# Last matrix products and their sums in halves, gate by a sigmoid on ScalarE, and the first tile's gather of 38 rows as 36 and 2

## Chip, cores and metric

One Trainium2 chip, one of its cores. The metric is the device time in microseconds of one execution; smaller is better. A measurement gives the median of several runs.

## What is computed

The kernel is one block of a vision transformer over 32 images of 36 patches, with 2 class rows ahead of each image's patches: 38 rows of 256 values an image. Cut to what matters here, for the second half of the block (`xn` is the normalised input, twice over):

```python
abel_out = gelu(xn @ abel_w + abel_b)
logits = xn @ moe_gate_w + moe_gate_b
topw, topi = top_k(logits, 2); topw = softmax(topw)
eo = gelu(xn @ ew1[e] + eb1[e]) @ ew2[e] + eb2[e]        # for the two experts of a row
moe_out = sum of topw * eo
for i in range(3):
    moe_out = moe_out @ expm(gens[i])                    # 256 x 256 rotations
gate = sigmoid(concat([abel_out, moe_out]) @ gc_w + gc_b)
out = residual + abel_out * (1 - gate) + moe_out * gate
```

## The kernel before

All engines run programs of their own, written out by hand and tied by semaphores; the order on each engine is the order of its code. The rows are cut into 11 tiles (`NT`) of 3 images, 114 rows; the last tile has 2 images, 76 rows. The class rows are alike in every image, so they are computed once, with image 0.

The work comes in stages: embedding of the patches, attention, the expert choice, and then 25 slots (`NS`) of 128 rows, each for one expert. GpSimd gathers a slot's rows, PE multiplies by the expert's two matrices, VectorE adds the bias (L1230), and GpSimd scatters the result to `y_rows` in HBM (L510). Beside the slots the three matrix exponentials are computed by polynomial and repeated squaring, in the buffers `Y` and `YT` (transposed), each 128 x 512: two row blocks of 256 columns.

The change touches what comes behind the slots. There:

- **SP** (L385 to L408) waits until all slots' results are in `y_rows`, then issues the gathers into `qk_sb` (L396): one per image, in order of tiles, 32 in all. Each takes 36 rows of 2 KB, both experts' results side by side, save image 0, whose transfer takes all 38 rows. Each tile has a semaphore `d_gather[t]`. Behind the last gather SP issues the outputs: for tile t it waits for `out_set` and issues a transfer per image (L401), and after tile 0 one more (L407) that writes the class rows of the other 31 images. Those are 33. At the end SP waits for all of them.
- **PE** finishes the exponentials by four products in a row (L1685 to L1690, the function `product`, whose matrix instructions have line L1559): the last square of exponential 2 into bank 4, the last square of exponential 1 (held transposed) into bank 0, their product into bank 4, and its product with exponential 0 into bank 5. Each is 4 matrix instructions, 8 passes in the profile, since 32-bit values take two. Then, per tile, `turn_moe` (L1698) transposes the weighed rows into bank 0 or 1, and `rotate` (L1709, L1711) multiplies by the product of the exponentials into one of banks 2 to 5 and subtracts `abel_out`. A 257th column gives the gate's argument; for tile 0 it is made by two more instructions (L1716), because `rotate(0)` begins before that column is set.
- **VectorE** adds, in `rotation` (L1244 to L1262): the two squares (L1245, L1248), the first product's sum (L1252), then the second weighing of tile 0's rows (`weigh_both`, L1288), the last sum into `ywide_sb` (L1256), and the gate column (L1260). Then, per tile, in `rotated`: it bounds the gate's argument (L1296), weighs the rows of tile t + 3 (L1288), and after ScalarE's exponential adds 1 and inverts (L1300, L1301), and computes `gate * (moe - abel) + (residual + abel)` (L1302).
- **ScalarE** loads the table of the exponential (L763), weighs the first expert's rows (`weigh_first`, L766) of tiles 0, 1 and 2, copies tile 0's transposed rows out of PSUM (`keep_moeT`, L755), and then goes round per tile: weigh tile t + 3, copy tile t + 1, exponential for the gate of tile t (L760).

## Time and profile before

| | us |
|---|---|
| runs | 341.42, 341.82, 345.4 |
| median | 341.82 |
| profiled execution, its own time | 344.48 |
| its span, first to last instruction | 341.6 |
| PE busy | 317.0 (93%) |
| VectorE busy | 209.5 (61%) |
| ScalarE busy | 183.4 (54%) |
| GpSimd busy | 148.4 (43%) |

The span leaves out 2.88 us of the profiled execution that lie around it. Busy times are sums over the whole span; issuing a DMA doesn't count as busy, so SP has no share there, and its queue is to be seen in the timeline only, as `SPq`. A mean granted TensorE clock of 0.989 stands beside this span.

### The profile page before, as it was taken

Reading aid. Unit: us, or ns where it says so; the run is one execution under the profiler, and the core shown is the slowest. Engines: PE = TensorE matmul, PEld = TensorE weight load, DVE = VectorE, ACT = ScalarE, POOL = GpSimd, SP = SyncE. Lnnn points to the kernel's source line nnn. Section 1 sums busy time; section 2 is a strip of 40 time slices with the busy share of each in tenths; the row PEclk is TensorE's granted clock in tenths of the full one; section 3 lists DMA queues with packets and bytes.
Section 4 is the critical chain, followed back from the end, with each engine's and each line's share of the span. In section 5 each row is a group of like instructions: output and inputs, shape, how many; then the busy total and the mean of one; then the engine's idle time right before and its main releaser. Section 6 shows DMA issues by size and latency. Waiting matters only on the chain.

```text
span 341.6 us, 6400 instructions
## 1 busy us (share of the span) xinstructions
PE 317.0 (93%) x1944; PEld 267.8 (78%) x1944; DVE 209.5 (61%) x576; ACT 183.4 (54%) x427; POOL 148.4 (43%) x152
## 2 busy tenths in 40 slices
PE   5999899999796999989999899999999999998894
PEld 4888455578685998876788788899998999896682
DVE  0146668599999688898877468776312231113684
ACT  0111454899798479975662594243443655550451
POOL 2002547133888468583002267857761654422000
PEclk9999999999999699999999999999999999999999
DMA  7940511124111111008834366636352466632632
GB/s 233 359 165 8 225 59 56 54 72 157 46 47 46 47 45 45 18 2 308 327 132 133 97 186 177 178 111 179 118 180 77 142 197 220 188 107 86 178 110 82
DMA packets 19219, 44.40 MB, mean 130 GB/s; under 512 B 2549, under 2 KB 11316, under 8 KB 18934
## 3 DMA queue, kind: packets, MB, share of 16 engines
q1 hardware_dynamic: 16790, 37.48, 33.8%
q0 software_dynamic: 2400, 6.56, 6.1%
q8 instruction: 15, 0.25, 0.3%
q14 instruction: 14, 0.11, 0.1%
HBM read 36.94 MB, written 7.09 MB: 129 GB/s over the span
## 4 chain that ended last, share of the span: by engine, by line
PE 75%; DVE 13%; DMA 3%; issue 3%; ACT 2%; POOL 1%; SPq 1%; DVEq 0%; POOLq 0%; ACTq 0%
PE banks L1611 11%; PE banks L1620 10%; PE banks L1559 10%; PE banks L1322 8%; PE banks L1459 5%; PE banks L1363 4%; PE banks L1435 4%; PE banks L1709 3%; PE banks L1477 2%; PE banks L1407 2%; PE banks L1421 2%; PE banks L1530 2%; PE banks L1368 2%; DVE kc_sb L917 2%; DVE qk_sb L1179 2%
## 5 line engine op out<-in xcount | busy, mean ns | idle before, releaser
L1611 PE MATMUL banks<-qn_sb,w_sb 128*128 128x128 f32 x400 | 49.1, 276 | 1.6 <-issue 0.8
L1611 PEld LDWEIGHTS banks<-qn_sb,w_sb 128*128 128x128 f32 x400 | 46.7, 192 | 2.4 <-issue 1.5
L1620 PE MATMUL banks<-w_sb,sq_sb 128*128 x200 | 47.1, 379 | 0.0
L694 ACT ACTIVATE qn_sb<-banks,col_sb 128x128 f32<-128x128 f32 x50 | 20.2, 457 | 44.2 <-PE banks L1598 44.2
L504 POOL DMA_INDIRECT qn_sb<-z_rows,gidx_sb x25 | 26.9, 1076 | 35.9 <-DVE gidx_sb L1133 18.9
L510 POOL DMA_INDIRECT y_rows<-pT_sb,sidx_sb x25 | 24.8, 991 | 39.8 <-DVE pT_sb L1230 38.9
L1230 DVE TENSOR_TENSOR pT_sb<-banks,p_sb 128x256 f32<-128x256 f32 x25 | 10.6, 424 | 49.7 <-PE banks L1620 46.9
L1620 PEld LDWEIGHTS banks<-w_sb,sq_sb 128*128 128x128 f32 x200 | 36.7, 190 | 4.3
L705 ACT ACTIVATE sq_sb<-banks,col_sb 128x128 f32<-128x128 f32 x100 | 31.2, 366 | 12.6 <-PE banks L1611 12.3
L592 ACT ACTIVATE kc_sb<-banks,col_sb 32x152 f32<-32x152 f32 x66 | 31.0, 470 | 1.1
L1322 PE MATMUL banks<-patch_sb,wtok_sb 128*128 128x252 f32 (+1 forms) x120 | 26.9, 388 | 3.7 <-DMA wtok_sb<-in_w_tok 3.7
L1322 PEld LDWEIGHTS banks<-patch_sb,wtok_sb 128*128 128x128 f32 x120 | 23.1, 207 | 6.7 <-DMA wtok_sb<-in_w_tok 4.0
L917 DVE TENSOR_SCALAR kc_sb<-banks,col_sb 32x152 f32<-32x152 f32 x66 | 25.6, 424 | 2.9 <-PE banks L1421 2.4
L297 POOL TENSOR_TENSOR qn_sb<-qk_sb,wtok_sb 114x768 f32<-114x768 f32 x11 | 17.1, 1556 | 14.7 <-DVE wtok_sb L892 7.6
L1459 PEld LDWEIGHTS banks<-vd_sb,pT_sb 114*114 114x114 f32 x132 | 18.3, 184 | 6.1 <-issue 5.4
L1459 PE MATMUL banks<-vd_sb,pT_sb 114*114 114x147 f32 x132 | 20.7, 300 | 2.1 <-ACT pT_sb L606 2.1
L583 ACT ACTIVATE qd_sb<-banks,col_sb 32x304 f32<-32x304 f32 x33 | 19.7, 597 | 4.0 <-PE banks L1407 3.6
L1363 PE MATMUL banks<-wqkv_sb,h_sb 128*114 128x512 f32 x44 | 20.8, 594 | 0.5 <-DVE wqkv_sb L838 0.5
L1435 PE MATMUL banks<-kc_sb,qd_sb 96*114 96x76 f32 x176 | 20.5, 262 | 0.0
L1435 PEld LDWEIGHTS banks<-kc_sb,qd_sb 96*114 96x114 f32 x176 | 20.4, 184 | 0.0
L474 POOL TENSOR_TENSOR att_sb<-p_sb 114x256 f32<-114x256 f32 x11 | 8.2, 745 | 25.8 <-DVE p_sb L970 25.8
L463 POOL TENSOR_TENSOR vd_sb<-vrep_sb,con_sb 114x768 f32<-114x768 f32 x11 | 17.1, 1551 | 0.0
(235 smaller groups left out, 632.1 us busy)
## 6 DMA issues: line engine op xcount, KB each, us to landing
w_sb<-in_w SPq DMA_DIRECT2D x25, 512.0 KB, 3.8
w_sb<-in_w SPq DMA_DIRECT2D x1, 4096.0 KB, 12.4
vrep_sb<-v_rows SPq DMA_DIRECT2D x33, 114.0 KB
qk_sb<-y_rows SPq DMA_DIRECT2D x31, 72.0 KB
patch_sb<-in_patches SPq DMA_DIRECT2D x2, 756.0 KB, 5.6
patch_sb<-in_patches SPq DMA_DIRECT2D x5, 252.0 KB, 4.4
v_rows<-v_sb SPq DMA_DIRECT2D x11, 114.0 KB
z_rows<-h_sb SPq DMA_DIRECT2D x11, 114.0 KB
```

The costliest lines, as they stand in the source:

```text
L504: pool.indirect_dma_start(out=xs_sb[:, s * D:(s + 1) * D], out_offset=None, in_=z_dram, in_offset=bass.IndirectOffsetOnAxis(ap=gidx_sb[:, ...
L510: pool.indirect_dma_start(out=y_dram, out_offset=bass.IndirectOffsetOnAxis(ap=sidx_sb[:, j:j + 1], axis=0), in_=ys_sb[:, s * D:(s + 1) * D ...
L592: last = nc.scalar.activation(kc[:, :, a, :], bank[2][r, :].rearrange("p (n m) -> p n m", m=128)[:, :, c], ACT.Identity, scale=col_sb[r, C ...
L705: last = nc.scalar.activation(hidT_sb[:, s * HID + c * 128:s * HID + (c + 1) * 128], bank[2 + 2 * s + c // 2][:, (c % 2) * 128:(c % 2 + 1) ...
L917: last = nc.vector.tensor_scalar(kc[:, :, a, :], bank[3][r, :].rearrange("p (n m) -> p n m", m=128)[:, :, c], col_sb[r, C_GK + a:C_GK + a ...
L1322: return nc.tensor.matmul(embed_out(g, c), wtok_sb[:, k * D + c * 128:k * D + (c + 1) * 128], patch_sb[:, at + k * w:at + (k + 1) * w], st ...
L1363: last = nc.tensor.matmul(bank[4 + s][0:T, :], hT(t, k), wqkv_sb[:, k * 3 * D:k * 3 * D + 2 * D], start=(k == 0), stop=(k == 1))
L1435: last = nc.tensor.matmul(bank[4 + hf][0:T, n * 2 * SEQ:(n + 1) * 2 * SEQ], qd_sb[0:96, q0:q0 + T], kc_sb[0:96, k0:k0 + 2 * SEQ], start=Fa ...
L1459: last = nc.tensor.matmul(bank[6 + n // 3][0:T, n % 3 * IPT * VW:(n % 3 * IPT + w) * VW], pT_sb[0:w * SEQ, n * T:(n + 1) * T], vd_sb[0:w * ...
L1559: last = nc.tensor.matmul(dst[:, m * D:(m + 1) * D], xT[:, k * D + m * 128:k * D + (m + 1) * 128], y[:, k * D:(k + 1) * D], start=(k == 0) ...
L1611: last = nc.tensor.matmul(bank[2 + 2 * s + c // 2][:, (c % 2) * 128:(c % 2 + 1) * 128], w1_sb[:, w0:w0 + 128], xsT_sb[:, (2 * s + k) * 128 ...
L1620: last = nc.tensor.matmul(bank[6 + s][:, 0:D], hidT_sb[:, s * HID + k * 128:s * HID + (k + 1) * 128], w2_sb[:, ds(e * 4 * D + k * D, D)], ...
```

## The change

In the gathers, image 0 gets a transfer of 36 rows as the others have, and its two class rows come by a transfer of their own behind tile 0's third; `d_gather[0]` is waited for with one transfer more. The second of the four products, the third and the fourth are made in halves of 256 columns, each half in a bank of its own (0 and 1, 4 and 5, 2 and 3), and each half's sum on VectorE follows its half; the sum of the second product goes to a free buffer, `YT[2]`. ScalarE copies tile 0's transposed rows ahead of the weighing of tile 2. The gate is one sigmoid on ScalarE, which reads its argument in PSUM and adds the other part as a bias; VectorE's bounding, adding and inverting are gone. `rotate(0)` waits for each half of `ywide_sb` by itself. The names of semaphores change with this (the declarations are left out below).

```diff
--- before.py
+++ after.py
@@ -392,8 +391,10 @@
 
             for t in range(NT):
                 for i in range(images(t)):
-                    r0, r1 = own_rows(t, i)
+                    r0, r1 = i * SEQ + NC, (i + 1) * SEQ
                     sp.dma_start(qk_sb[r0:r1, t * 2 * D:(t + 1) * 2 * D], y2[t * T + r0 + 1:t * T + r1 + 1, :]).then_inc(d_gather[t], 16)
+                if t == 0:
+                    sp.dma_start(qk_sb[0:NC, 0:2 * D], y2[1:NC + 1, :]).then_inc(d_gather[0], 16)
 
             def out_tile(t):
                 for i in range(images(t)):
@@ -754,28 +755,29 @@
                 act.wait_ge(moe_turned, t + 1)
                 nc.scalar.activation(xT_sb[:, s * 2 * T:(s + 1) * 2 * T], bank[s][:, 0:2 * T], ACT.Copy).then_inc(moeT_set, 1)
 
-            def gate_exp(t):
+            def gate(t):
                 n = real(t)
-                act.wait_ge(z_bounded, t + 1)
-                nc.scalar.activation(z_sb[0:n, 2 * NT + t:2 * NT + t + 1], z_sb[0:n, NT + t:NT + t + 1], ACT.Exp,
-                                     scale=-1.0).then_inc(gexp_set, 1)
-
-            nc.scalar.activation(al_sb[:, 77:78], con_sb[:, K_ZERO:K_ZERO + 1], ACT.Exp).then_inc(exp_warm, 1)
+                act.wait_ge(rot_made, t + 1)
+                nc.scalar.activation(z_sb[0:n, NT + t:NT + t + 1], bank[2 + t % 4][0:n, D:D + 1], ACT.Sigmoid,
+                                     bias=z_sb[0:n, t:t + 1]).then_inc(gate_set, 1)
+
+            nc.scalar.activation(al_sb[:, 77:78], con_sb[:, K_ZERO:K_ZERO + 1], ACT.Sigmoid)
             def weigh_first(t):
-                act.wait_ge(d_gather[t], 16 * images(t))
+                act.wait_ge(d_gather[t], 16 * (images(t) + (t == 0)))
                 nc.scalar.activation(expert_rows(t, 0), expert_rows(t, 0), ACT.Copy,
                                      scale=wt_sb[0:real(t), 2 * NT + t:2 * NT + t + 1]).then_inc(first_set, 1)
 
             act.wait_ge(resid_set, 1)
-            for t in range(3):
-                weigh_first(t)
+            weigh_first(0)
+            weigh_first(1)
             keep_moeT(0)
+            weigh_first(2)
             for t in range(NT):
                 if t + 3 < NT:
                     weigh_first(t + 3)
                 if t + 1 < NT:
                     keep_moeT(t + 1)
-                gate_exp(t)
+                gate(t)
 
         @block.vector
         def _(dve):
@@ -1244,22 +1246,25 @@
                 dve.wait_ge(s_made, 3 * more + 2)
                 nc.vector.scalar_tensor_tensor(out=Y[0], in0=Y[0], scalar=2.0, in1=bank[4][:, :], op0=ALU.mult,
                                                op1=ALU.add).then_inc(s_kept_cr, 1)
-                dve.wait_ge(s_made, 3 * more + 3)
-                nc.vector.scalar_tensor_tensor(out=YT[1], in0=YT[1], scalar=2.0, in1=bank[0][:, :], op0=ALU.mult,
-                                               op1=ALU.add).then_inc(s_kept_cr, 1)
-                dve.wait_ge(s_kept_cr, 3 * more + G + 3)
-                dve.wait_ge(e_made, 1)
-                nc.vector.tensor_tensor(Y[1], Y[0], bank[4][:, :], ALU.add).then_inc(e_kept, 1)
+                half = [slice(m * D, (m + 1) * D) for m in range(2)]
+                for m in range(2):
+                    dve.wait_ge(s_made, 3 * more + 3 + m)
+                    nc.vector.scalar_tensor_tensor(out=YT[2][:, half[m]], in0=YT[1][:, half[m]], scalar=2.0, in1=bank[m][:, 0:D],
+                                                   op0=ALU.mult, op1=ALU.add).then_inc(s_kept_cr, 1)
+                dve.wait_ge(s_kept_cr, 3 * more + G + 4)
+                for m in range(2):
+                    dve.wait_ge(e_made, m + 1)
+                    nc.vector.tensor_tensor(Y[1][:, half[m]], Y[0][:, half[m]], bank[4 + m][:, 0:D], ALU.add).then_inc(e_kept, 1)
                 weigh_both(0)
-                dve.wait_ge(e_kept, 1)
-                dve.wait_ge(e_made, 2)
-                nc.vector.tensor_tensor(yw3[:, :, 0:D], Y[1].rearrange("p (k d) -> p k d", k=2),
-                                        bank[5][:, :].rearrange("p (k d) -> p k d", k=2), ALU.add).then_inc(e_widened, 1)
-                dve.wait_ge(e_widened, 1)
+                for m in range(2):
+                    dve.wait_ge(e_kept, m + 1)
+                    dve.wait_ge(e_made, m + 3)
+                    nc.vector.tensor_tensor(yw3[:, m, 0:D], Y[1][:, half[m]], bank[2 + m][:, 0:D], ALU.add).then_inc(e_widened, 1)
+                dve.wait_ge(e_widened, 2)
                 for k in range(2):
                     nc.vector.tensor_tensor_reduce(att_sb[:, 0:D], yw3[:, k, 0:D], row_sb[:, R_GW + D:R_GW + 2 * D], 1.0, 0.0,
                                                    ALU.mult, ALU.add, yw3[:, k, D:D + 1]).then_inc(e_widened, 1)
-                    dve.wait_ge(e_widened, k + 2)
+                    dve.wait_ge(e_widened, k + 3)
 
             for j in range(NS):
                 if P0_AT <= j < P0_AT + G:
@@ -1290,15 +1295,10 @@
 
             def rotated(t):
                 n, b = real(t), bank[2 + t % 4]
-                zt = z_sb[0:n, NT + t:NT + t + 1]
-                g = z_sb[0:n, 3 * NT + t:3 * NT + t + 1]
-                dve.wait_ge(rot_made, t + 1)
-                nc.vector.tensor_scalar(zt, b[0:n, D:D + 1], z_sb[0:n, t:t + 1], -87.0, ALU.add, ALU.max).then_inc(z_bounded, 1)
+                g = z_sb[0:n, NT + t:NT + t + 1]
                 if t + 3 < NT:
                     weigh_both(t + 3)
-                dve.wait_ge(gexp_set, t + 1)
-                link(nc.vector.tensor_scalar(g, z_sb[0:n, 2 * NT + t:2 * NT + t + 1], 1.0, None, ALU.add))
-                link(nc.vector.reciprocal(g, g))
+                dve.wait_ge(gate_set, t + 1)
                 nc.vector.scalar_tensor_tensor(out=h1_sb[0:n, t * D:(t + 1) * D], in0=b[0:n, 0:D], scalar=g, in1=hb_sb[0:n, t * D:(t + 1) * D],
                                                op0=ALU.mult, op1=ALU.add).then_inc(out_set, 1)
 
@@ -1683,11 +1683,26 @@
 
             pe.wait_ge(s_evac, 3 * more + 3)
             product(bank[4], YT[2], Y[2]).then_inc(s_made, 1)
-            product(bank[0], Y[1], YT[1]).then_inc(s_made, 1)
+
+            def half_product(dst, xT, y, m, k):
+                return nc.tensor.matmul(dst[:, 0:D], xT[:, k * D + m * 128:k * D + (m + 1) * 128], y[:, k * D:(k + 1) * D],
+                                        start=(k == 0), stop=(k == 1))
+
+            for m in range(2):
+                half_product(bank[m], Y[1], YT[1], m, 0)
+                half_product(bank[m], Y[1], YT[1], m, 1).then_inc(s_made, 1)
             pe.wait_ge(s_kept_cr, 3 * more + G + 3)
-            product(bank[4], YT[1], Y[0]).then_inc(e_made, 1)
+            half_product(bank[4], YT[2], Y[0], 0, 0)
+            pe.wait_ge(s_kept_cr, 3 * more + G + 4)
+            half_product(bank[4], YT[2], Y[0], 0, 1).then_inc(e_made, 1)
+            half_product(bank[5], YT[2], Y[0], 1, 0)
+            half_product(bank[5], YT[2], Y[0], 1, 1).then_inc(e_made, 1)
             pe.wait_ge(e_kept, 1)
-            product(bank[5], YT[0], Y[1]).then_inc(e_made, 1)
+            half_product(bank[2], YT[0], Y[1], 0, 0)
+            pe.wait_ge(e_kept, 2)
+            half_product(bank[2], YT[0], Y[1], 0, 1).then_inc(e_made, 1)
+            half_product(bank[3], YT[0], Y[1], 1, 0)
+            half_product(bank[3], YT[0], Y[1], 1, 1).then_inc(e_made, 1)
 
             def turn_moe(t):
                 n, s = real(t), t % 2
@@ -1706,12 +1721,14 @@
                     pe.wait_ge(out_set, t - 3)
                 w = D if t == 0 else D + 1
                 for k in range(2):
+                    if t == 0:
+                        pe.wait_ge(e_widened, k + 1)
                     nc.tensor.matmul(b[0:n, 0:w], xT_sb[:, (2 * s + k) * T:(2 * s + k) * T + n],
                                      ywide_sb[:, k * (D + 2):k * (D + 2) + w], start=(k == 0), stop=False, skip_group_check=True)
                 last = nc.tensor.matmul(b[0:n, 0:D], minus_sb[0:n, 0:n], h_sb[0:n, t * D:(t + 1) * D], start=False, stop=True,
                                         skip_group_check=True)
                 if t == 0:
-                    pe.wait_ge(e_widened, 3)
+                    pe.wait_ge(e_widened, 4)
                     for k in range(2):
                         last = nc.tensor.matmul(b[0:n, D:D + 1], xT_sb[:, (2 * s + k) * T:(2 * s + k) * T + n],
                                                 ywide_sb[:, k * (D + 2) + D:k * (D + 2) + D + 1], start=(k == 0), stop=(k == 1),
@@ -1720,7 +1737,6 @@
 
             pe.wait_ge(minus_set, 1)
             turn_moe(0)
-            pe.wait_ge(e_widened, 1)
             rotate(0)
             turn_moe(1)
             for t in range(1, NT):
```

How the instructions stand, by engine. **SP** behind the slots, before (`qk_sb` takes the gathered rows, `out_rows` is the output; the first three rows are the loop that loads expert weights):

```order
L374 DMA w_sb<-in_w 128x1024
L263 REGISTER_ALU
L263 COMPARE_AND_BRANCH
L396 DMA qk_sb<-y_rows 38x512
L396 DMA qk_sb<-y_rows 36x512 x31
L401 DMA out_rows<-h_sb 38x256
L401 DMA out_rows<-h_sb 36x256 x2
L407 DMA out_rows<-h_sb 2x31x256
L401 DMA out_rows<-h_sb 36x256 x29
```

and now:

```order
L373 DMA w_sb<-in_w 128x1024
L262 REGISTER_ALU
L262 COMPARE_AND_BRANCH
L395 DMA qk_sb<-y_rows 36x512 x3
L397 DMA qk_sb<-y_rows 2x512
L395 DMA qk_sb<-y_rows 36x512 x29
L402 DMA out_rows<-h_sb 38x256
L402 DMA out_rows<-h_sb 36x256 x2
L408 DMA out_rows<-h_sb 2x31x256
L402 DMA out_rows<-h_sb 36x256 x29
```

There are 66 transfers in place of 65; everything behind tile 0's third gather stands one place later.

**PE** at the third and fourth product, before (`p_sb` and `wtok_sb` hold `Y` and `YT`):

```order
L1559 MATMUL banks<-wtok_sb,p_sb 128x256 x4
L1687 REGISTER_ALU
L1559 MATMUL banks<-p_sb,wtok_sb 128x256 [waits s_kept_cr]
L1559 MATMUL banks<-p_sb,wtok_sb 128x256 x3
L1559 MATMUL banks<-p_sb,wtok_sb 128x256 [waits e_kept]
L1559 MATMUL banks<-p_sb,wtok_sb 128x256 x3
L1698 MATMUL banks<-con_sb,qk_sb 128x114 [waits both_set,minus_set]
```

and now:

```order
L1688 MATMUL banks<-wtok_sb,p_sb 128x256 x4
L1694 REGISTER_ALU
L1688 MATMUL banks<-p_sb,wtok_sb 128x256 [waits s_kept_cr]
L1696 REGISTER_ALU
L1688 MATMUL banks<-p_sb,wtok_sb 128x256 [waits s_kept_cr]
L1688 MATMUL banks<-p_sb,wtok_sb 128x256 x2
L1688 MATMUL banks<-p_sb,wtok_sb 128x256 [waits e_kept] x2
L1688 MATMUL banks<-p_sb,wtok_sb 128x256 x2
L1713 MATMUL banks<-con_sb,qk_sb 128x114 [waits both_set,minus_set]
```

The matrix instructions are as many as before; the waits are for halves, and there are two more of them.

**ScalarE** behind the table load, before (`d_gather` are the gathers of a tile, `z_sb` holds the gate's numbers, `xT_sb` the transposed rows):

```order
L763 ACT_TABLE_LOAD
L763 ACTIVATE al_sb<-con_sb 128x1
L766 ACTIVATE qk_sb<-qk_sb,wt_sb 114x256 [waits d_gather0,resid_set]
L766 ACTIVATE qk_sb<-qk_sb,wt_sb 114x256 [waits d_gather1]
L766 ACTIVATE qk_sb<-qk_sb,wt_sb 114x256 [waits d_gather2]
L755 ACTIVATE xT_sb<-banks 128x228 [waits moe_turned]
L766 ACTIVATE qk_sb<-qk_sb,wt_sb 114x256 [waits d_gather3]
L755 ACTIVATE xT_sb<-banks 128x228 [waits moe_turned]
L760 ACTIVATE z_sb<-z_sb 114x1 [waits z_bounded]
```

and now:

```order
L764 ACT_TABLE_LOAD
L764 ACTIVATE al_sb<-con_sb 128x1
L767 ACTIVATE qk_sb<-qk_sb,wt_sb 114x256 [waits d_gather0,resid_set]
L767 ACTIVATE qk_sb<-qk_sb,wt_sb 114x256 [waits d_gather1]
L756 ACTIVATE xT_sb<-banks 128x228 [waits moe_turned]
L767 ACTIVATE qk_sb<-qk_sb,wt_sb 114x256 [waits d_gather2]
L767 ACTIVATE qk_sb<-qk_sb,wt_sb 114x256 [waits d_gather3]
L756 ACTIVATE xT_sb<-banks 128x228 [waits moe_turned]
L761 ACTIVATE z_sb<-banks,z_sb 114x1 [waits rot_made]
```

The copy of tile 0's transposed rows stands one place earlier, and the gate's instruction waits for PE's `rot_made` where it waited for VectorE's `z_bounded`. One table load stands there as before.

## Rows read from the trace of the kernel before

**Rows 1.** Timeline of SP's queue from 305 us: start us, us, engine line op.

```profile
312.32 13.23 SPq L396 DMA_DIRECT2D qk_sb<-y_rows  x32
325.60 1.01 SPq L401 DMA_DIRECT2D out_rows<-h_sb  x3
326.65 0.28 SPq L407 DMA_DIRECT2D out_rows<-h_sb  x1
326.98 13.14 SPq L401 DMA_DIRECT2D out_rows<-h_sb  x29
```

**Rows 2.** The same timeline in narrow windows, so that single DMA issues show.

```profile
313.03 0.35 SPq L396 DMA_DIRECT2D qk_sb<-y_rows  x1
313.43 0.37 SPq L396 DMA_DIRECT2D qk_sb<-y_rows  x1
321.18 0.70 SPq L396 DMA_DIRECT2D qk_sb<-y_rows  x1
325.60 0.26 SPq L401 DMA_DIRECT2D out_rows<-h_sb  x1
327.76 1.23 SPq L401 DMA_DIRECT2D out_rows<-h_sb  x1
329.04 0.85 SPq L401 DMA_DIRECT2D out_rows<-h_sb  x1
339.34 0.36 SPq L401 DMA_DIRECT2D out_rows<-h_sb  x1
339.76 0.35 SPq L401 DMA_DIRECT2D out_rows<-h_sb  x1
```

**Rows 3.** Waits of SP's queue from 300 us: total us, times, longest us.

```profile
SPq L71 <- DMA out_rows<-h_sb: 1.1, 1, 1.1
```

**Rows 4.** The chain that ended last, pieces in order: start us, us, what.

```profile
309.92 2.39 DMA y_rows<-pT_sb,sidx_sb
315.47 2.88 DMA qk_sb<-y_rows
319.27 1.09 PE banks L1709 x4
337.54 0.48 DVE h_sb L1302
```

**Rows 5.** Timeline of the last products and of the first tiles' weighing.

```profile
310.64 1.89 PE L1559 MATMUL banks<-wtok_sb,p_sb 128*128 128x256 f32 x8
313.31 1.99 PE L1559 MATMUL banks<-p_sb,wtok_sb 128*128 128x256 f32 x8 [0.78 <-DVE wtok_sb L1248]
316.15 1.99 PE L1559 MATMUL banks<-p_sb,wtok_sb 128*128 128x256 f32 x8 [0.85 <-DVE p_sb L1252]
316.95 0.51 ACT L766 ACTIVATE qk_sb<-qk_sb,wt_sb 114x256 f32<-114x256 f32 x1 [9.06 <-DMA qk_sb<-y_rows]
317.69 0.51 ACT L766 ACTIVATE qk_sb<-qk_sb,wt_sb 114x256 f32<-114x256 f32 x1 [0.23 <-DMA qk_sb<-y_rows]
```

**Rows 6.** Groups of instructions by form, 307 to 342 us: busy us, mean ns.

```profile
L1302 DVE SCALAR_TENSOR_TENSOR h_sb<-banks,z_sb,hb_sb 114x256 f32<-114x256 f32 x10 | 4.8, 485 | 0.3
L1296 DVE TENSOR_SCALAR z_sb<-banks,z_sb 114x1 f32<-114x1 f32 x10 | 2.2, 218 | 1.9 <-PE banks L1711 0.7 <-PE banks L1716 0.3
L760 ACT ACTIVATE z_sb<-z_sb 114x1 f32<-114x1 f32 x10 | 2.0, 202 | 7.2 <-DVE z_sb L1296 7.2
L1300 DVE TENSOR_SCALAR z_sb<-z_sb 114x1 f32<-114x1 f32 x10 | 1.5, 149 | 0.7 <-ACT z_sb L760 0.5
L1301 DVE RECIPROCAL z_sb<-z_sb 114x1 f32<-114x1 f32 x10 | 1.6, 164 | 0.3
L1230 DVE TENSOR_TENSOR pT_sb<-banks,p_sb 128x256 f32<-128x256 f32 x2 | 0.8, 424 | 4.0 <-PE banks L1620 4.0
```

**Rows 7.** Windows: us, busy us of each engine, granted clock, DMA share, GB/s.

```profile
115.00:120.00 5.00, 5.00 (x34) 5.00 (x33) 3.54 (x9) 3.56 (x7) 3.79 (x4) 0.61 0.16 50
325.00:333.00 8.00, 8.00 (x44) 6.54 (x43) 7.11 (x28) 4.57 (x17) 0.00 (x0) 1.00 0.37 106
```

More of the change, by code:

```diff
@@ L221, in vit_kernel @@
         gap_set, ratio_set, resid_set, abelw_set = sem("gap_set"), sem("ratio_set"), sem("resid_set"), sem("abelw_set")
-        zrow_set, hit_set, ruler_set, m_made, exp_warm, where_set = (
-            sem("zrow_set"), sem("hit_set"), sem("ruler_set"), sem("m_made"), sem("exp_warm"), sem("where_set"))
+        zrow_set, hit_set, ruler_set, m_made, where_set = (
+            sem("zrow_set"), sem("hit_set"), sem("ruler_set"), sem("m_made"), sem("where_set"))
         residual_set, placed, onep_set, minus_set, e_widened = sem("residual_set"), sem("placed"), sem("onep_set"), sem("minus_set"), sem("e_widened")
@@ L230, in vit_kernel @@
         bound_set, counted, more_set = sem("bound_set"), sem("counted"), sem("more_set")
-        z_bounded = sem("z_bounded")
         poly_set, stats_done = sem("poly_set"), sem("stats_done")
@@ L238, in vit_kernel @@
         moe_turned, moeT_set, rot_made = sem("moe_turned"), sem("moeT_set"), sem("rot_made")
-        gexp_set, out_set = sem("gexp_set"), sem("out_set")
+        gate_set, out_set = sem("gate_set"), sem("out_set")
         ident = con_sb[:, K_ID:K_ID + 128]
```

## The prediction

> **What bounds the kernel now.** The page gives PE 93% of the span, but this change touches only what comes behind the expert slots, so I read the end of the trace alone, in this order: the chain of waits, SP's queue, the timeline, the groups by form, the granted clock.
>
> The chain of waits leads from the last scatter, landed 2.39 us after 309.92, over gathers and PE to the last gated sum on VectorE, 337.54 plus 0.48, so 338.02 [rows 4]. It ends there, because it follows busy instructions only. The span is 341.6 us. What lies between is SP's. SP issues 32 gathers from 312.32 and then 33 output transfers, the last from 339.76 to 340.11 [rows 1, 2]. It then waits 1.1 us for the last one to land [rows 3]: 341.2, and some 0.4 us of ending.
>
> Is SP waiting for results there, or is it the bound? Look at where its pieces meet: gathers end at 312.32 + 13.23 = 325.55 and the first output starts at 325.60; the four pieces follow one another within 0.05 us down to the last [rows 1]. Tile 10, the last tile, has two images, and their issues start at 339.34 and 339.76 [rows 2], while its values were there at 338.02 [rows 4]: SP came 1.3 us late. So from 312.32 on the kernel ends when SP has got through 65 issues; PE, VectorE and ScalarE run beside that with 1.3 us to spare.
>
> SP's pace: 339.76 - 312.32 = 27.44 us for 64 steps. Three issues are long, 0.70, 1.23 and 0.85 us against 0.37 of an ordinary one [rows 2], 1.67 us too much together. (27.44 - 1.67) / 64 = 0.40 us a step, as 313.03 to 313.43 shows too [rows 2].
>
> **The change part by part.**
>
> *Gathers.* The first transfer of 38 rows becomes one of 36, and one of 2 rows is added behind tile 0's third. SP has 66 issues in place of 65. A 2-row gather is not in the trace. The nearest rows are the first output, 38 rows, 0.26 us, and the output for the repeated class rows, whose slowest dimension is 2 too, 0.28 us [rows 1, 2]; an ordinary gather is 0.37 [rows 2]. With 0.05 us between issues the step costs 0.31 to 0.42. The first transfer, now of 36 rows, can cost up to 0.06 more. Bounds +0.31 and +0.48; I take **+0.36**, nearer to the row with dimension 2. Nothing covers it: every later issue moves back by as much.
>
> *When the gathers land.* Tile 0 is weighed at 316.95, 3.9 us after its third issue began at 313.03; tile 1 at 317.69, and the ninth gather, begun 315.47, needed 2.88 [rows 2, 4, 5]. With the 2-row transfer beginning at 313.43 and 2.4 (the scatter's landing) to 2.9 us of flight, tile 0 is there at 315.8 to 316.3, about 0.8 us sooner. Tile 1's last is now the seventh, from about 314.6: 317.0 to 317.5; if it keeps tile 1's present delay it is 318.1.
>
> The trace says that the 38-row transfer was slow to land and the 36-row ones not. The Trainium skill, "DMA: Bandwidth & Descriptors", section "Why a DMA increments its semaphore by 16 and not by 1", states that a transfer spreads over the largest count up to 16 that divides its rows: 38 over 2 engines, 36 over 12. By that rule, the trace agrees. The same page speaks against the change in "Rules for kernel authors": two transfers to disjoint partitions serialize, don't bother. By the one tile 0 comes earlier, by the other up to 0.4 us later; neither alters the sum, because the end is SP's.
>
> *Products in halves.* Before, each sum waits for eight passes: products at 310.64, 313.31 and 316.15, 1.89 to 1.99 us each, with 0.8 us of idle PE ahead of the last two [rows 5]. Now the first half of the 310.64 product is there by 311.7, its sum of 256 columns costs 0.48 (as the gated sum) [rows 6], so by 312.2, before PE has issued the second half at 312.4. A pass is about 1.89 / 8 = 0.22 us apart from the next. The second half's sum is done by 313.05; the next product has issued its first two passes by then and needs six more, 1.3 us, to 314.4. Its sums of 0.42 each [rows 6] end at 314.1 and 315.0, and the last product, six passes and 0.15 us of draining behind the second sum, at about 316.5 in place of 316.15 + 1.99 = 318.14 [rows 5]. So the products gain 1.6 us, which rotate(0) can't use, since tile 0's rows come later than they end.
>
> *Weighing order.* Tile 0's copy out of PSUM stands behind two weighings now, not three. Queued: weighing of tile 1 from 317.5 to 318.0 (0.51) [rows 5], then the copy. Today rotate(0) begins 0.4 us after the weighing ahead of the copy (315.47 + 2.88 + 0.51 = 318.86, and 319.27) [rows 4, 5]. So it begins at about 318.4: 0.9 us earlier. Range 0.3 (tile 1 at 318.1) to 1.3. On VectorE the two wide sums stand behind weigh_both(0), which waits for tile 0 until 316.8, so they end at 318.2, in time.
>
> *Gate.* Per tile VectorE loses three small operations, 0.22, 0.15 and 0.16 us, and ScalarE's 0.20 us [rows 6] becomes a sigmoid that reads PSUM and a bias. Not in the trace; bounds 0.20 (the exp) and 0.51 (256 columns, scaled) [rows 5, 6]; I take 0.25. In the middle tiles this is worth nothing, because PE is busy 8.00 of 8.00 us there [rows 7]. Behind the last tile it takes about 0.5 us off. There is one table load behind the slots in both kernels.
>
> **Sum.** The last gated sum moves from 338.02 to 338.02 - 0.9 - 0.5 = 336.6. SP gets to tile 10 at 339.34 + 0.36 = 339.7, 3.1 us later. All 1.4 us gained are hidden behind SP, and what remains is +0.36: span 341.96, the profiled execution 344.48 + 0.36 = 344.84. That execution was a long one. The runs are 341.42, 341.82 and 345.4, so executions differ by 3 to 4 us; in the profiled one the clock stood at 0.61 from 115 to 120 us with PE busy throughout [rows 7], which costs about 2 us in those 5 alone. I add the 0.36 to the median: 341.82 + 0.36 = **342.2 us**.
>
> **Rivals.**
>
> *A: the queue's long issues go as well.* For it: with the 38-row gather gone, two DMA engines carry less, and the 0.70 us issue may have waited on them. Against: the 1.23 and 0.85 us issues come right behind the 38-row and the 2 x 31-row output, which stay. Price: -0.33 for the first, -1.67 for all: 341.85 to 340.5. By the Trainium skill's rule on the number of engines, first named above, it would be the first alone.
>
> *B: compute sets the end after all* (the 65 issues only look back to back, and some wait for VectorE's sums). Then -1.4 counts: 340.4. Against: 1.3 us of lag at tile 10.
>
> *C: slower.* The fuller PE behind the slots makes its clock fall as it fell at 115 us [rows 7]. From 318.4 PE has some 17 us of work; at 0.61 it takes 17 x (1 / 0.61 - 1) = 10.9 us longer, less the 3.1 us to spare, plus 0.36: +8.2, so 350. It decides once the clock is under 17 / (17 + 3.1) = 0.85. Against: it stood at 1.00 with PE fully busy from 325 to 333 [rows 7].
>
> *D: it does not do what it says,* tile 1 or tile 0 landing late as before: rotate(0) gains nothing, but the end is still SP's, 342.2 too; it is part of the forecast. A new long issue like the 0.85 one would add 0.5: 342.7.
>
> **How the numbers follow.** Forecast, including D: 0.72. A: 0.15. B: 0.08. C: 0.02. The rest, 0.03, is of unknown cause within a few us. Mechanisms alone give 340.4 to 342.7; but whichever level most of the runs fall on moves a median of few by 3 us, and the upper run of before, 345.4, is as much to be had. Hence 341.0 to 345.0. A measurement of this kernel tells about 2%, 6.8 us, from no change: faster needs under 335, which no case gives, 0.01; slower needs C, 0.02; within 2%, 0.97.
>
> **What would show it right or wrong.** Right: 66 issues back to back, the first output 0.3 to 0.4 us later than 325.60, the last issue near 340.1; the last gated sum at about 336.6; PE's last product ending near 316.5 and rotate(0) at 318.4; VectorE's L1302 with idle time. Wrong: SP's last issue before 339.76 (A, by which of the three long ones is missing), gaps between SP's outputs that end with VectorE's sums (B), a granted clock under 0.85 behind 318 us (C).

## The result and the profile after

The changed kernel took 347.48 us (median of 4 runs, 347.07 to 350.97), the kernel before 343.61 us (median of 4, 341.42 to 346.0): a ratio of 1.0132, 95% interval 1.007 to 1.0193. The difference is under the 2% that counts as faster or slower, but the time lies outside the forecast range of 341.0 to 345.0. Ratios here and below compare the executions of each kernel that are within 1.5% of its own fastest, so they are not the ratios of the medians beside them. In the profiled execution (347.07 us, span 345.2) two things are longer, and they have nothing to do with each other.

**The head.** SP's first gather is issued at 314.45, before at 312.32 [rows 1]. Nothing ahead of it was changed. These are the windows of the changed kernel's attention stage (columns as in [rows 7]):

```profile
80.00:90.00 10.00, 8.51 (x59) 7.55 (x58) 9.63 (x23) 7.09 (x15) 5.77 (x5) 0.82 0.40 132
90.00:100.00 10.00, 10.00 (x76) 9.42 (x75) 7.98 (x23) 8.15 (x18) 6.15 (x7) 0.84 0.14 45
100.00:110.00 10.00, 9.52 (x84) 8.56 (x82) 9.23 (x28) 9.25 (x20) 8.64 (x9) 1.00 0.15 48
110.00:120.00 10.00, 7.79 (x39) 7.27 (x39) 7.32 (x21) 5.18 (x12) 5.10 (x5) 0.68 0.14 47
120.00:130.00 10.00, 9.84 (x83) 9.12 (x82) 8.37 (x23) 8.13 (x18) 6.77 (x7) 0.98 0.14 45
```

Read the third number from the right, the clock granted to PE, as a share of full speed. It fell twice here. In the profile before the same five windows stand at 1.00 but for this one:

```profile
110.00:120.00 10.00, 9.28 (x51) 8.76 (x52) 7.21 (x20) 4.94 (x10) 5.00 (x5) 0.66 0.15 47
```

Multiply what is missing by 10 us each: 1.8 + 1.6 + 3.2 + 0.2 = 6.8 us at full clock, against 3.4 in the profile before. This sum is called "clock lost" below. The head is 2.1 us longer.

**The tail.** From the first gather's issue to the end of the span: 341.6 - 312.32 = 29.28 us before, 345.2 - 314.45 = 30.75 now. SP's queue (compare [rows 1, 2]):

```profile
314.45 1.14 SPq L395 DMA_DIRECT2D qk_sb<-y_rows  x3
315.63 0.26 SPq L397 DMA_DIRECT2D qk_sb<-y_rows  x1
315.93 11.95 SPq L395 DMA_DIRECT2D qk_sb<-y_rows  x29
327.92 1.01 SPq L402 DMA_DIRECT2D out_rows<-h_sb  x3
328.97 0.27 SPq L408 DMA_DIRECT2D out_rows<-h_sb  x1
329.28 14.46 SPq L402 DMA_DIRECT2D out_rows<-h_sb  x29
```

and single issues in it:

```profile
330.09 1.03 SPq L402 DMA_DIRECT2D out_rows<-h_sb  x1
331.17 0.99 SPq L402 DMA_DIRECT2D out_rows<-h_sb  x1
333.84 1.73 SPq L402 DMA_DIRECT2D out_rows<-h_sb  x1
343.38 0.36 SPq L402 DMA_DIRECT2D out_rows<-h_sb  x1
```

The pieces follow each other within 0.05 us from 314.45 to 343.74, as before. So the 2-row issue takes 0.26 + 0.04 us, and the long issues exceed 0.37 by 2.84 us together (those three and one of 0.57) where before it was 1.67. The span is 345.2 - 341.96 = 3.2 us over the forecast one: 2.1 of head and 1.2 of longer issues, less 0.06 because the added issue was cheaper than forecast.

What VectorE, PE and ScalarE do meanwhile (timeline; [rows 4, 5]):

```profile
314.49 4.32 PE L1688 MATMUL banks<-p_sb,wtok_sb 128*128 128x256 f32 x16
317.35 0.51 ACT L767 ACTIVATE qk_sb<-qk_sb,wt_sb 114x256 f32<-114x256 f32 x1 [7.33 <-DMA qk_sb<-y_rows]
318.85 0.51 ACT L767 ACTIVATE qk_sb<-qk_sb,wt_sb 114x256 f32<-114x256 f32 x1 [0.99 <-DMA qk_sb<-y_rows]
319.65 1.12 PE L1726 MATMUL banks<-ywide_sb,xT_sb 128*114 128x256 f32 x4 [0.65 <-ACT xT_sb L756]
337.60 0.48 DVE L1302 SCALAR_TENSOR_TENSOR h_sb<-banks,z_sb,hb_sb 76x256 f32<-76x256 f32 x1 [0.82 <-ACT z_sb L761]
```

Set each against its own first gather. Tile 0 is weighed 2.90 us after it (before 4.63), rotate(0) begins after 5.20 (6.95), the last gated sum ends after 338.08 - 314.45 = 23.63 (25.70). Compute is 2.1 us quicker, and SP issues the last image 5.3 us after its values are there. By form, behind the slots [rows 6]:

```profile
L1302 DVE SCALAR_TENSOR_TENSOR h_sb<-banks,z_sb,hb_sb 114x256 f32<-114x256 f32 x10 | 4.8, 484 | 5.9 <-ACT z_sb L761 5.9
L761 ACT ACTIVATE z_sb<-banks,z_sb 114x1 f32<-114x1 f32 x10 | 2.6, 261 | 5.7 <-PE banks L1728 5.7
L1252 DVE SCALAR_TENSOR_TENSOR wtok_sb<-wtok_sb,banks 128x256 f32<-128x256 f32 x2 | 0.8, 421 | 0.6 <-PE banks L1688 0.6
```

### The profile page after: what moved, and what is told of

It is laid out like the page before. It is cut to its first block, busy times and chain, and to the rows that moved or that the text cites. A ratio compares the mean times of both kernels' runs of the same rounds, so it can differ in the third digit from the quotient of the medians.

```text
span 345.2 us, 6373 instructions
## 1 busy us (share of the span) xinstructions
PE 320.0 (93%) x1944; PEld 270.0 (78%) x1944; DVE 206.0 (60%) x546; ACT 184.2 (53%) x427; POOL 148.2 (43%) x152
## 4 chain that ended last, share of the span: by engine, by line
PE 73%; DVE 10%; DMA 6%; issue 3%; ACT 3%; SPq 2%; POOL 1%; POOLq 0%; DVEq 0%; ACTq 0%
PE banks L1611 11%; PE banks L1620 10%; PE banks L1559 8%; PE banks L1322 7%; PE banks L1459 6%; PE banks L1363 4%; PE banks L1435 4%; DMA qn_sb<-z_rows,gidx_sb 4%; PE banks L1407 3%; PE banks L1726 3%; PE banks L1421 2%; PE banks L1477 2%; PE banks L1530 2%; PE banks L1368 2%; PE banks L1598 2%
## 5 line engine op out<-in xcount | busy, mean ns | idle before, releaser
L1322 PEld LDWEIGHTS banks<-patch_sb,wtok_sb 128*128 128x128 f32 x120 | 22.1, 201 | 6.9 <-DMA wtok_sb<-in_w_tok 4.7
L1459 PEld LDWEIGHTS banks<-vd_sb,pT_sb 114*114 114x114 f32 x132 | 19.4, 194 | 6.7 <-issue 6.0
L1459 PE MATMUL banks<-vd_sb,pT_sb 114*114 114x147 f32 x132 | 22.1, 313 | 2.5 <-ACT pT_sb L607 2.5
L475 POOL TENSOR_TENSOR att_sb<-p_sb 114x256 f32<-114x256 f32 x11 | 8.2, 744 | 28.5 <-DVE p_sb L972 28.5
```

The costliest lines, as they stand in the source:

```text
L1322: return nc.tensor.matmul(embed_out(g, c), wtok_sb[:, k * D + c * 128:k * D + (c + 1) * 128], patch_sb[:, at + k * w:at + (k + 1) * w], st ...
L1459: last = nc.tensor.matmul(bank[6 + n // 3][0:T, n % 3 * IPT * VW:(n % 3 * IPT + w) * VW], pT_sb[0:w * SEQ, n * T:(n + 1) * T], vd_sb[0:w * ...
```

## The experiments

Theory Q: the tail ends when SP has issued everything; the change adds one issue of 0.3 us, and what compute gains is hidden. Theory H: the difference in the head is the clock's and differs between executions of one kernel. Rivals: the change itself slows the head or SP's other issues; PE and VectorE set the end. Each tail below is that of one profiled execution. The kernels have names: ctl_before and ctl_after are the two kernels again ("its copy"); after_38 and before_36_2 change the gather split alone; after_no_cls and after_pool_cls change the output of the class rows; after_4more makes SP's queue longer; after_pool_outs, before_pool_outs, after_shared, after_shared2 and after_three_queues make it shorter, each with its own share for the other engines. "Tail" below is from the first gather's issue to the end of the last output's issue on SP's queue, "net" is the tail less what its long issues exceed 0.37 us by.

### Both kernels again

No edit.

> The kernel before, unchanged, timed against itself. Theory Q (SP's queue): the tail from the first gather's issue to the last output's is 27.4 us again give or take its long issues (1.67 us too much before), ratio 1.000. Theory H (head): executions of one kernel differ by 3 to 4 us because the TensorE clock is below 1 in the attention stage in some, so the same kernel gives runs from 341 to 346 and its span goes with that clock. If H holds for this code too, the ratio's interval holds 1 and is some 0.5% wide.

Measured: ratio 1.0019 (0.9978 to 1.006); 12 runs from 341.48 to 347.66, and 35 runs of the kernel before beside it from 340.87 to 350.88. Tail 27.77 us.

> The changed kernel again. Theory Q: first gather to last output 28.93 us in its first profile, 1.49 us more than before: 0.32 of it the added issue and the rest longer issues. If that is the change's, it is 28.5 to 29.3 here; if long issues are a matter of chance, it is anywhere from 27.8 up. Theory H: the rest of the difference (2.1 us at the first gather) is clock, and it will not come back: ratio 1.003 to 1.005. If the change itself slows the head, the ratio is again near 1.013.

Measured: ratio 0.9987 (0.9936 to 1.0038), median 343.38, 12 runs from 342.09 to 351.19. Tail 28.53 us, last sum at 334.10, 23.49 us after the first gather. The attention stage of the two profiles, the copy of before first:

```profile
80.00:90.00 10.00, 7.01 (x62) 6.22 (x60) 9.59 (x25) 7.53 (x17) 5.91 (x5) 1.00 0.37 126
90.00:100.00 10.00, 9.77 (x55) 9.08 (x56) 6.23 (x18) 6.47 (x15) 5.78 (x5) 0.66 0.14 45
110.00:120.00 10.00, 7.30 (x33) 6.24 (x33) 7.40 (x18) 4.49 (x11) 3.96 (x3) 0.62 0.14 45
120.00:130.00 10.00, 9.85 (x77) 9.27 (x75) 7.33 (x20) 7.69 (x16) 6.75 (x7) 0.87 0.14 46
```

```profile
80.00:90.00 10.00, 8.57 (x59) 7.83 (x59) 9.59 (x25) 7.46 (x16) 5.90 (x5) 0.79 0.38 125
90.00:100.00 10.00, 10.00 (x79) 9.43 (x77) 8.04 (x22) 8.17 (x18) 6.64 (x7) 0.87 0.14 45
110.00:120.00 10.00, 8.49 (x66) 7.58 (x67) 9.38 (x25) 7.05 (x15) 6.04 (x6) 1.00 0.15 47
```

Here it is the kernel before that loses more clock, 8.5 us against 3.4, and its first gather comes at 316.50, the changed kernel's at 310.61. Over the 14 profiles of this study the loss between 80 and 130 us, summed as above, and the first gather's issue go together, whatever the code:

| clock lost, us | first gather at, us |
|---|---|
| 1.7 | 309.56, 309.87, 310.35, 310.48 |
| 3.4 | 310.61, 311.36, 312.32 (before), 312.60 |
| 6.8 | 314.45 (after), 316.1 |
| 8.5 | 316.50, 318.32 |
| 10.2 | 318.60, 318.86 |

One microsecond of lost clock costs about one; at the same loss the head still differs by up to 2 us, whatever the code. The spans and mean granted clocks of all executions say the same. Over the 110 executions of the kernel before with both on record, the clock lies between 0.964 and 0.994, and 0.01 less goes with 3.1 us more of span; single executions scatter by 0.8 us about that straight line. The changed kernel's executions lie on it or a little below: the four of the first measurement by 0.5 us, the 12 of the second by 0.4, with standard errors of 0.2 and 0.3. H holds: the 1.3% of the first measurement is not the change's, and the repeated one shows no difference.

### The gather split alone, both ways

```diff
-                    r0, r1 = i * SEQ + NC, (i + 1) * SEQ
+                    r0, r1 = own_rows(t, i)
...
-                if t == 0:
-                    sp.dma_start(qk_sb[0:NC, 0:2 * D], y2[1:NC + 1, :]).then_inc(d_gather[0], 16)
...
-                act.wait_ge(d_gather[t], 16 * (images(t) + (t == 0)))
+                act.wait_ge(d_gather[t], 16 * images(t))
```

> The changed kernel with image 0 gathered by one transfer of 38 rows again, so 65 issues. Theory Q: 0.3 us faster than the changed kernel by the issue alone, 1.5 us faster (tail 27.4 us) if the split also lengthens other issues. Rival: the split is worth nothing either way because PE and VectorE set the end; then no difference, and the last output waits for VectorE.

Measured: ratio 1.0022 (0.9966 to 1.0078). Tail 29.50, long issues 3.33 too much, net 26.17 us; tile 0 weighed after 4.12, last sum after 24.32. No difference in time is measured, as is to be expected of 0.3 us against an interval of some 2 us either way; what follows rests on the profiles.

The reverse, the split put into the kernel before:

> The kernel before with only the gather split made. Theory Q: 66 issues; tail longer by one step of 0.3 us (27.8 to 28.1 us at like long issues), tile 0 weighed 2.9 us after the first gather in place of 4.6, the last sum hardly sooner, since the copy still stands behind the weighing of tile 2 (it ends 0.4 us later if anything). Rival (the 38-row transfer also holds up the later ones): tile 1 and 2 are weighed 1 us sooner too, and the last sum comes 0.5 us or more sooner.

Measured, in one profile: tail 28.01, long issues 1.55, net 26.46. ScalarE's weighings, with the first gather at 310.48:

```profile
313.53 0.51 ACT L768 ACTIVATE qk_sb<-qk_sb,wt_sb 114x256 f32<-114x256 f32 x1 [7.48 <-DMA qk_sb<-y_rows]
315.01 0.51 ACT L768 ACTIVATE qk_sb<-qk_sb,wt_sb 114x256 f32<-114x256 f32 x1 [0.98 <-DMA qk_sb<-y_rows]
316.31 0.51 ACT L768 ACTIVATE qk_sb<-qk_sb,wt_sb 114x256 f32<-114x256 f32 x1 [0.79 <-DMA qk_sb<-y_rows]
```

Tile 0 after 3.05, tile 1 after 4.53 (before 5.37), tile 2 after 5.83 (6.05), the last sum after 25.48 (25.70). The net tails settle the price: 26.13, 26.16 and 26.17 us in the three profiles with 65 issues and the 38-row gather (before, its copy, after_38), 26.45, 26.43 and 26.46 in the three with 66 (after, its copy, this one). The split costs 0.3 us of queue, and no other step became longer; the rest is long issues. The rival on tiles 1 and 2 holds in part: tile 1 gains 0.8, the end 0.2.

### What the long issues are

```diff
-                if t == 0:
-                    sp.dma_start(out.rearrange("(b j) d -> j b d", j=SEQ)[0:NC, 1:B, :],
-                                 h1_sb[0:NC, 0:D].unsqueeze(1).broadcast_to([NC, B - 1, D])).then_inc(d_out, 16)
...
```

> The changed kernel without the output of the class rows of images 1 to 31 (31 x 2 rows of 1 KB left unwritten). Theory Q with the long issues caused by this transfer, which has few engines: all long issues behind the first outputs go, 2.64 us and the issue's own 0.31, so 3 us faster than the changed kernel. If the long issues have another cause (code fetch, any full queue), only 0.3 us goes. Rival (compute sets the end): 0.

Measured: ratio 0.9911 (0.9849 to 0.9972), for a kernel that leaves out part of the output. The long issues right behind that transfer are gone: the 39th and 40th before (excess 1.34 us together), one of 1.70 us in its copy (1.33), the 40th and 41st after (1.28) and in its copy (1.89). One long issue stays, the 53rd, 1.95 us; tail 27.75. So the class rows' transfer accounts for 1.3 to 1.9 us, not for all the long issues, and the 1.73 us issue of the changed kernel has another cause. The DMA view of the changed kernel from 333.5 to 334.5 shows what goes with it:

```profile
q1 hardware_dynamic: 125, 0.10, 33.8%
q8 instruction: 1, 0.02, 8.3%
```

A packet passes on a queue that the profile calls "instruction" just as SP stands still. Six profiles have such a q8 packet behind the first output (the changed kernel, after_38, after_no_cls, after_pool_cls, after_4more, after_shared2), and all six have a lone long issue of 1.3 to 2.2 us within 0.2 us of it; the copy of the changed kernel, with the same code, has neither before its span ends. That SP waits for this packet, as for code, is the likely reading, but no run changed the packets alone, and what decides whether one comes was not tried.

The first of the three long issues before, 0.70 us at 321.18, has its own such packet, on the other instruction queue. From 320.9 to 321.7 the DMA view of the kernel before has:

```profile
q14 instruction: 1, 0.01, 5.5%
```

Seven profiles have an issue of 0.5 to 0.7 us among the gathers, ahead of the class rows, each 0.04 to 0.24 us behind the start of a q14 packet. Two of them are the changed kernel's, and before_36_2 has one too (0.57 us), so it does not hang on the 38-row gather.

The same output issued by GpSimd, as soon as tile 0's values are there (SP's part of the edit is the one above):

> The changed kernel with only the class rows of images 1 to 31 output from GpSimd. Theory Q with the long issues behind the first outputs caused by that transfer on SP's queue: they go (1.3 to 1.9 us), and the issue itself (0.31): tail from first gather to last output 26.6 us if no code fetch falls into it, 28 to 28.4 if one does. Rival (the transfer is slow wherever it is issued, and SP's issues wait for the same DMA engines): the long issues stay, tail 28.2.

Measured: ratio 1.0022 (0.998 to 1.0065), tail 28.35, net 26.14 with 65 issues on SP. SP has a 1.61 us issue at 321.55, among its gathers, 1.5 us after GpSimd issued the class rows, and one of 1.34 beside a q8 packet. The rival holds: the class rows' transfer holds up SP's issues whoever issues it. All six profiles in which GpSimd issues it have a long issue of SP that starts 0.6 to 1.5 us after GpSimd has issued it. Whether SP waits for the same DMA engines, as the rival says, no run shows.

### The queue made longer

```diff
+                if t == 5:
+                    for n in range(4):
+                        sp.dma_start(v_dram[n * SEQ + NC:(n + 1) * SEQ, :], h1_sb[NC:SEQ, 0:D]).then_inc(d_out, 16)
...
```

> The changed kernel with four more transfers of 36 rows issued by SP behind the outputs of tile 5 (tile 0's rows into a scratch tensor that nothing reads; outputs unchanged). Theory Q: 70 issues, the last output's issue ends 4 x 0.41 = 1.6 us later at like long issues: 30.1 us after the first gather with a long class-row transfer alone (28.5 in the one profile that has no code fetch behind the first output), 31 with a code fetch too; last sum unmoved at 23.5 to 24.4. Rival (compute or the transfers themselves set the end): 28.5 to 29.3 as before.

SP's queue behind the class rows, and the last sum (first gather at 318.32):

```profile
333.06 9.60 SPq L402 DMA_DIRECT2D out_rows<-h_sb  x15
342.70 1.59 SPq L412 DMA_DIRECT2D v_rows<-h_sb  x4
344.33 5.95 SPq L402 DMA_DIRECT2D out_rows<-h_sb  x14
```

```profile
341.29 0.48 DVE L1305 SCALAR_TENSOR_TENSOR h_sb<-banks,z_sb,hb_sb 76x256 f32<-76x256 f32 x1 [0.82 <-ACT z_sb L764]
```

In one profile: tail 31.96, long issues 3.59, a gap of 0.37 ahead of the last issue (its cause is open): 28.00 net of both, 1.56 more than 26.44, so 0.39 for each issue, all of it in the end. The last sum stands where it stood, 23.45 us after the first gather; the last output's issue ends 8.5 us behind it. This excludes compute as the bound.

### The queue made shorter

GpSimd issues the class rows and the outputs of tiles 0, 3 and 6 (the same code in all the kernels of this part, with other tiles):

```diff
...
             for t in range(NT):
+                if t in (0, 3, 6):
+                    continue
                 sp.wait_ge(out_set, t + 1)
...
+            for t in pool_tiles:
+                pool.wait_ge(out_set, t + 1)
+                for i in range(images(t)):
+                    r0, r1 = i * SEQ + (0 if t == 0 and i == 0 else NC), (i + 1) * SEQ
+                    pool.dma_start(out[t * T + r0:t * T + r1, :], h1_sb[r0:r1, t * D:(t + 1) * D]).then_inc(d_cls, 16)
```

> The changed kernel with the outputs of tiles 0, 3 and 6 and the class rows issued by GpSimd, which is idle there: SP has 56 issues in place of 66. Theory Q: SP's queue no longer sets the end; its gathers end 13.1 us after the first, 23 outputs take 9.4, and the last tile's two outputs follow its sum (23.5 us after the first gather in two profiles) within 0.1 us: last output issued 24.4 us after the first gather's issue, span end 25.9 us after it, against 30.0 to 30.8 now; 4 to 5 us faster. Rival (compute or the transfers set the end): no gain; outputs landing late behind GpSimd's, 2 us or more of waiting at the end.

Measured: ratio 0.9969 (0.9922 to 1.0016). Span 338.4, first gather 311.36: 27.0 us to the end, against 29.99 in the copy of the changed kernel and 30.75 in its first profile. SP waits for VectorE's sums ahead of each of the last four tiles; the last sum comes after 24.31. So SP's queue is no longer the bound there, but the gain is 3 to 3.7 us of tail where 4 to 5 were expected, and in the times it is under what they resolve. 0.8 us of the miss is the later last sum (tile 7 weighed after 13.85, in the changed kernel after 12.6 to 12.7), and about 0.5 is the end of the program, which GpSimd sets here. SP's last wait is longer than the 0.2 us of the kernel before, and what GpSimd does then is shown with after_shared2 below:

```profile
SPq L71 <- PEq L71: 0.7, 1, 0.7
```

> The kernel before with the same outputs moved to GpSimd. Theory Q: here the last tile's sum comes 25.7 us after the first gather's issue (two profiles), so the span ends 28.1 us after it, 1.2 us sooner than now, and the changed kernel with the same move is 2.2 us faster than this one: the change's gain shows once the queue is out of the way. Rival (the change's compute gain is not real): both alike.

Measured: ratio 0.9998 (0.996 to 1.0036); 344.6 - 316.10 = 28.5 us to the end, last sum after 25.64. With the same queue the changed kernel is 1.5 us ahead of this one in the profiles (2.2 expected). The ratios don't tell the two apart. At the same mean clock the changed one's 12 executions are 0.9 us under the line of the kernel before, and the 12 of before_pool_outs are on it (standard errors 0.3 and 0.2). So the gain shows once SP is out of the way.

GpSimd issues every third tile's gathers too, beginning with tile 1's:

> The changed kernel with GpSimd issuing the gathers of tiles 1, 4, 7 and 10 and the outputs of tiles 0, 3, 6 and 9 and the class rows; SP has 22 gathers and 20 outputs. Theory Q and the landing of gathers: tile 1 is weighed 3.4 us after the first gather in place of 4.4, no tile waits for its rows later on, the last sum comes 23.2 us after the first gather (23.5 to 24.4 so far), the span ends 25.7 us after it (27.0 with outputs alone moved, 30 to 30.8 in the changed kernel). Rival (gathers are held by the DMA engines, not by their issue): tile 1 is weighed at 4 us or later, last sum 24.3, end 27.

> As after_shared, with tile 0's copy ahead of the weighing of tile 1. If the copy waits only for the transposes, rotate(0) begins 0.2 to 0.4 us sooner than in after_shared and the end comes as much sooner. Rival: the weighing of tile 1 is then late for tile 1's copy, and the end is the same.

Measured: ratios 1.0054 (1.0012 to 1.0097) and 1.005 (1.0006 to 1.0095): slower by 0.5%, where 4 us less tail was expected. Tile 1, gathered by GpSimd, was weighed 5.66 and 5.31 us after the first gather, later than the 4.40 of the changed kernel; the last sums came after 24.80 and 24.46. And the end is GpSimd's now. Its last outputs, and the wait at SP's end, of after_shared2 (SP's last issue ends at 335.07, the span at 342.8):

```profile
333.33 1.52 POOL L557 DMA_DIRECT2D out_rows<-h_sb  x3 [2.96 <-DVE h_sb L1320]
```

```profile
SPq L71 <- PEq L71: 6.1, 1, 6.1
```

From 334.85 to 342.8 it is 8.0 us, in after_shared 7.9. It is not the landing that takes so long. SP's own outputs, issued until 335.07, landed 1.4 us later, and GpSimd passed its wait for its own at 336.3. What then fills the time is an instruction that closes GpSimd's program (from the view of line 71: shortest, median and longest in ns, then the start in us):

```profile
L71 POOLq DRAIN  x1: 6108/6108/6108, 336.5 to 336.5; - x1
```

The same DRAIN is in every kernel: 5.4 us in the kernel before, where it runs from 309.7 beside everything else, 4.2 with the class rows alone on GpSimd, 5.0 with ten transfers, 6.1 in these two. It starts when GpSimd's last wait is over, so whatever GpSimd does late puts it behind the rest. In after_pool_outs and before_pool_outs too it ends last, 0.5 and 0.6 us behind SP.

Exchanging ScalarE's copy and the weighing brought rotate(0) 1.2 us forward against after_shared (after 5.26 in place of 6.47), but the last sum by 0.3 only.

So GpSimd must be done early, and its gathers given back. GpSimd issues the class rows and tiles 0, 2 and 4, and ScalarE the last image:

```diff
...
+            act.wait_ge(out_set, NT)
+            act.dma_start(out[(NT - 1) * T + SEQ + NC:(NT - 1) * T + 2 * SEQ, :],
+                          h1_sb[SEQ + NC:2 * SEQ, (NT - 1) * D:NT * D]).then_inc(d_last, 16)
...
```

> The changed kernel with the class rows and the outputs of tiles 0, 2 and 4 issued by GpSimd and the last image's output by ScalarE; SP has 55 issues. In the four profiles with GpSimd outputs the program ended 6.7 to 7.9 us after GpSimd's last issue, so here GpSimd must be done by 16.5 us after the first gather and does not set the end. Theory Q: the last sum comes 23.5 to 24.4 us after the first gather, the last two outputs are issued at once, the span ends 25.7 to 26.5 us after it, against 27.0 with tiles 0, 3, 6 and 30 to 30.8 in the changed kernel; time ratio to the kernel before 0.990 to 0.995 if the heads are alike. Rival: the class-row transfer holds SP's queue wherever it is issued (1.3 to 1.6 us so far), SP is then late for the last tile, 27 us.

Measured: **339.99 us** (339.1 to 340.93, 6 runs), ratio to the kernel before **0.9878** (0.9827 to 0.993), the only version here with the whole output that is measurably faster than before, though by less than 2%. SP's queue and ScalarE's output (first gather 309.56, last sum at 334.83, span 336.9):

```profile
320.02 1.32 SPq L395 DMA_DIRECT2D qk_sb<-y_rows  x1
324.80 10.37 SPq L402 DMA_DIRECT2D out_rows<-h_sb  x22
```

```profile
334.87 0.64 ACTq L791 DMA_DIRECT2D out_rows<-h_sb  x1
```

27.3 us to the end, not the 25.7 to 26.5 expected: the class rows, issued at 318.50 by GpSimd, held up SP's gathers (three issues, 1.88 us too much), tile 7 was weighed after 14.82 us in place of the changed kernel's 12.6 to 12.7, and the last sum came after 25.27. That is the rival's mechanism, at another place. The ratio is better than the 0.990 to 0.995 expected although the tail is worse, and that is luck: about half of the 1.2% is a good head: 1.7 us of clock lost in this profile, granted clocks of 0.990 to 0.995 in all 6 runs. At the same mean clock they are 2.1 us (standard error 0.2) under the line of the kernel before, and the tails differ by 29.28 - 27.3 = 2.0.

## Why the prediction was wrong in its number and right in its mechanism

- **SP's queue bounds the tail, and compute's gain is hidden.** Right, shown by four more issues (+1.56 us at an unmoved last sum, one profile) and by the shorter queues.
- **+0.36 us for the added issue.** Measured 0.30, just under the lower bound of 0.31: the 2-row issue was 0.26 + 0.04. The first transfer, where up to 0.06 more was allowed for, adds nothing that the net tails show.
- **The long issues stay at 1.67 us.** This term was mis-sized: 2.84 in the first profile, 2.10 in the second, 1.6 to 3.6 over the profiles in which SP issues all. The text bounded their growth by 0.5 us from one profile. They are mostly two things, what the class rows' transfer adds (1.3 to 2.1) and what goes with a q8 packet in some executions (1.0 to 1.8 over the ordinary 0.37). In the span this term put the profiled execution 1.2 us over the forecast.
- **"I add the 0.36 to the median: 341.82", with a range to 345.0.** This is the step that failed: the base of the sum, a median of three taken for the time of the head. Three runs do not show how far the heads of this kernel differ; 35 runs went from 340.87 to 350.88, with medians of 344.1 to 345.4 in the later measurements. I read one fall of the clock in one profile and took its cost for constant, with 345.4 as the far end. The loss was 1.7 to 10.2 us over the profiles, and the first gather came anywhere from 309.56 to 318.86. The 4 runs of the first measurement had granted clocks of 0.963 to 0.976 over the whole span; at those clocks the kernel before takes as long. Why all four were low there, and what makes the clock fall in the attention stage at all, is open.
- **Products in halves.** Last product to end 4.2 us after the first gather by the sum (316.5); measured 4.36. The first 256-column sum took 0.42, not 0.48. The pace of 0.22 us a pass was right, though 1.89 / 8 is 0.24: in the trace a pass begins 0.22 us after the one before it and the last ends 0.16 us late, and both are in the 1.89.
- **Landing of the gathers.** Tile 0 expected 3.5 to 4.0 us after the first gather, measured 2.9: the 2-row transfer was there 1.7 us after its issue began, less than the lower bound of 2.4, which came from a scatter into HBM. Hence rotate(0) gained 1.75 us where 0.9 was forecast, and the last sum 2.1 where 1.4 was.
- **Gate.** 0.26 us (0.25 taken); VectorE idles 5.9 us ahead of its sums. What it is worth by itself no run shows; from rotate(0) to the last sum it is 18.4 and 18.2 us in the changed kernel's two profiles and 18.75 in both of the kernel before, so about the 0.5 us forecast.
- **Rivals.** B (compute sets the end) fell with after_4more. C (a clock fall behind the slots) did not come: the clock stood at 1.00 from 318 us until PE's last product in both profiles of the changed kernel, and where it fell near the end of a span PE was idle. A's long issues did not go; the 0.70 us one was not the 38-row gather's, it came again as 0.57 and 0.58 in the changed kernel's two profiles.
- Tile 0 was weighed 1.2 to 1.7 us sooner with the split than without and tile 1 0.4 to 1.0, and the end pays 0.3 us. The Trainium skill's rule ("DMA: Bandwidth & Descriptors", "Why a DMA increments its semaphore by 16 and not by 1": 38 rows over 2 engines, 36 over 12) agrees with the landing; no view here shows the engines themselves. That page's advice "Don't bother — they serialize" ("Rules for kernel authors") is for two partition halves that both use all 16 engines, and it is not borne out for the landing of this pair.

## What to carry to other kernels

Lay the issues of the last stage end to end on the queue that issues them: where they follow without a gap, the chain of waits ends too early, and no faster engine helps until an issue is taken away. Before another engine gets some of them, look at what closes that engine's program. Before a forecast of less than 1%, look at how far runs of the same code differ and in which stage, and compare profiles from a point behind it.

## What the runs showed that was not expected

- A transfer of 31 x 2 rows of 1 KB, issued by GpSimd, lengthened issues on SP's queue by 1.2 to 1.9 us.
- The same code had a packet on an instruction queue in the output stage in one execution and none in the next; beside such a packet one issue took 1.3 to 2.2 us instead of 0.37, in six profiles of six.
- GpSimd's plain transfers took 0.5 us each to issue, and the program ended 8 us after the last of them in two profiles, where SP's end came 1.5 us after its last. 6.1 us of that was GpSimd's closing DRAIN, which takes 4.2 to 6.1 us in every kernel here and costs nothing while it runs beside other work.
- Tile 1 was weighed up to 1.3 us later when GpSimd issued its gathers beside SP's.
